# Order of the score blocks and the value projection inside the steps of two cross attentions

## The reference, cut to what matters

```
# second (l1x): masked, scaled dot products      # fourth (l3x): unit vectors and a bias
q, k, v = x@Wq, ctx@Wk, ctx@Wv                   q, k = l2norm(x@Wq + bq) * scale, l2norm(ctx@Wk)
w = where(mask, -1e10, q.k / 4)                  w = q.k + fside            # fside: 64 x 1601
out = softmax(w) @ v @ Wproj + b                 out = softmax(w) @ v @ Wo + b
```

## Time and profile before

| | us |
|---|---|
| median of 3 runs | 2484.82 (2483.24 to 2486.69) |
| the profiled execution, its own time | 2488.87 |
| span of the profiled execution | 2487.2 |
| second cross attention, batches in the loop | about 374 to 695 |
| fourth cross attention, batches in the loop | about 1838 to 2226 |

### The profile page before, as it was taken

How to read it: one execution, slowest core, us unless ns; L and a number is a source line. 1 busy time by engine, 2 the same in 40 slices (tenths; PEclk the granted TensorE clock), 3 DMA queues, 4 the chain that set the end, 5 groups by cost and what they waited for, 6 DMA issues and landing times. The chain is left out here.

```text
span 2487.2 us, 51006 instructions
## 1 busy us (share of the span) xinstructions
PE 2239.6 (90%) x20593; PEld 1421.5 (57%) x20650; DVE 1649.7 (66%) x3182; ACT 1243.9 (50%) x2071; POOL 814.2 (33%) x688
## 2 busy tenths in 40 slices
PE   8885879999978899999999999699879999998898
PEld 6764546666644555666655666356545555566554
DVE  6976365555549746888888854744676666665577
ACT  3335135555554235555555554576545555563565
POOL 5610052242208020332133300045545455443254
PEclk9998889999989989999999999899999999999999
DMA  4201363334231237666686663133322323220231
GB/s 118 73 1 47 100 167 91 95 86 120 54 135 38 47 99 144 132 137 125 141 155 124 115 117 69 34 108 102 110 67 72 83 74 82 68 67 23 72 96 60
DMA packets 358619, 226.84 MB, mean 91 GB/s; under 512 B 289913, under 2 KB 326611, under 8 KB 358387
## 3 DMA queue, kind: packets, MB, share of 16 engines
q1 hardware_dynamic: 355314, 215.20, 35.8%
q0 software_dynamic: 3072, 8.39, 1.2%
HBM read 114.87 MB, written 0.52 MB: 46 GB/s over the span
## 5 line engine op out<-in xcount | busy, mean ns | idle before, releaser
L3953 POOL TENSOR_TENSOR l2x_rows<-l2x_rows,l2x_one 128x256 f16<-128x256 f32 (+1 forms) x91 | 89.2, 1007 | 382.1 <-DVE l2x_rows L1507 354.6
L100 PE MATMUL PS<-hot 128*128 128x512 f16 x460 | 139.6, 441 | 82.4 <-DVE l0a_g L1119 17.5
L4057 PE MATMUL PS<-l2x_rows,l2x_pth 128*128 128x512 f16 x832 | 200.4, 379 | 1.9 <-DVE l2x_mean L4266 1.9
L3714 DVE CUSTOM_DVE_ANT_0 l1x_junk<-PS,l1x_bias 128x1024 bf16<-128x1024 f32 (+1 forms) x128 | 123.3, 992 | 74.3 <-PE PS L3374 73.4
L4259 DVE TENSOR_TENSOR l2x_pl<-l2x_sc,l2x_ph 128x1664 f16<-128x1664 f32 x64 | 125.1, 1954 | 44.6 <-ACT l2x_ph L4136 43.9
L4154 ACT ACTIVATE l2x_meanT<-PS 128x256 f32<-128x256 f32 x64 | 24.6, 384 | 250.3 <-PE PS L4019 250.3
L4244 DVE CUSTOM_DVE_ANT_0 l2x_sc<-PS,l2x_bias 128x1665 f32<-128x1665 f32 x64 | 120.9, 1889 | 38.5 <-issue 37.3
L3714 DVE CUSTOM_DVE_ANT_0 l3x_junk<-PS,l3x_bias 128x1024 bf16<-128x1024 f32 (+1 forms) x128 | 123.6, 991 | 24.2 <-PE PS L3374 21.2
L100 PEld LDWEIGHTS PS<-hot 128*128 128x128 f16 x460 | 45.8, 109 | 153.1 <-issue 39.8
L4011 PE MATMUL PS<-l2x_kh,l2x_qth 128*128 128x512 f16 (+1 forms) x512 | 131.9, 339 | 1.5 <-issue 1.5
L4011 PE MATMUL PS<-l2x_kl,l2x_qth 128*128 128x512 f16 (+1 forms) x512 | 131.9, 339 | 0.0
(11 more groups left out here) (866 smaller groups left out, 6119.4 us busy)
## 6 DMA issues: line engine op xcount, KB each, us to landing
l2f_unit<-in_L_ffn_units_dram SPq DMA_DIRECT2D x36, 384.0 KB, 3.1
l3f_unit<-in_L_ffn_units_dram SPq DMA_DIRECT2D x34, 384.0 KB, 3.1
l1x_kst<-l1x_kh SPq DMA_DIRECT2D x128, 100.1 KB, 2.2
l3x_kst<-l3x_kh SPq DMA_DIRECT2D x128, 100.1 KB, 2.2
l2x_rows<-in_ctx_dram SPq DMA_DIRECT2D x8, 1536.0 KB
l1x_ctx<-in_ctx_t_dram SPq DMA_DIRECT2D x7, 1601.0 KB, 7.6
l3x_ctx<-in_ctx_t_dram SPq DMA_DIRECT2D x7, 1601.0 KB, 7.9
l1x_kst<-l1x_kl SPq DMA_DIRECT2D x64, 100.1 KB, 2.2
```

The lines of the kernel that those rows point to most:

```text
L100: self.nc.tensor.matmul(self.PS[:, bank, :], self.hot[:, 0:P], self.hot[:], start=True, stop=True)
L3714: v.tensor_tensor_reduce(junk[:, slot(it), 0:n], slot_banks(it)[:, 0:n], bias[:, 0 if normed else b % 2, at:at + n], 1.0, LOWEST, ALU.add, ...
L3953: last = nc.gpsimd.tensor_tensor(high[:, at], of[:, at], one[0:p, at].unsqueeze(2).unsqueeze(3).to_broadcast([p, i, NC, P]), ALU.mult)
L4057: nc.tensor.matmul(PS[:, ACC, :], pth[:, u % 2, m, :], rows2[:, b % 2, :, :, m, :], start=(m == 0), stop=False)
```

## The change

The lists of steps are edited, nothing else. In the second attention three pairs [V, A] become [A, V] (steps 10, 13, 16) and [M 0, A10] becomes [A10, M 0] (step 18). In the fourth, A2 moves from step 13 into step 14 ahead of V3, A4 moves from step 15 to step 16, and [M 0, A10] becomes [A10, M 0] (step 20). No instruction is added or removed.

```
     if normed:
...
-                 [P_, A[0], ("U", 1, 1)], [A[1], A[2]], [("V", 3, 0)], [A[3], A[4]], [A[5]], [A[6]], [A[7], A[8]],
-                 [A[9]], [("M", 0, 0), A[10]], [A[11]], [A[12]], [A[13], A[14]], [A[15]], [("M", 1, 0)]]
+                 [P_, A[0], ("U", 1, 1)], [A[1]], [A[2], ("V", 3, 0)], [A[3]], [A[4], A[5]], [A[6]], [A[7], A[8]],
+                 [A[9]], [A[10], ("M", 0, 0)], [A[11]], [A[12]], [A[13], A[14]], [A[15]], [("M", 1, 0)]]
...
     else:
...
-                 [("V", 1, 0), A[2]], [A[3]], [P_, A[4]], [("V", 2, 0), A[5]], [A[6]], [A[7]], [("V", 3, 0), A[8]], [A[9]],
-                 [("M", 0, 0), A[10]], [A[11]], [A[12]], [A[13]], [A[14]], [A[15]], [], [("M", 1, 0)]]
+                 [A[2], ("V", 1, 0)], [A[3]], [P_, A[4]], [A[5], ("V", 2, 0)], [A[6]], [A[7]], [A[8], ("V", 3, 0)], [A[9]],
+                 [A[10], ("M", 0, 0)], [A[11]], [A[12]], [A[13]], [A[14]], [A[15]], [], [("M", 1, 0)]]
```

## The result

| | us |
|---|---|
| before, median of 5 runs | 2484.82 (2483.24 to 2492.22) |
| changed, median of 5 runs | 2496.53 (2493.61 to 2501.92) |
| ratio changed to before | 1.0047, 95% interval 1.0033 to 1.0061 |
| forecast | 2494.5 (2482 to 2501) |

11.7 us were lost; 9.7 were forecast. The profiled execution of the changed kernel took 2501.92 us, the slowest of its five, so its span (2500.2 us) shows 13 us more and not 11.7.

The account below looks back on a forecast made before the run. The prediction took PE, busy 93 to 94%, as the bound. It added 4.4 us (second attention) and 5.3 us (fourth), 9.7 in all, to the median of 2484.8: 2494.5 us, range 2482 to 2501.

Parts of the forecast that it names:

- PE's waits set the pace: Both stages: PE is busy 93 to 94%, so the change is worth the change in PE's waits, no work being added.
- The 1.92 us from the start of a wide A to the next use of its slot: Both attentions: a wide A read by DVE holds its slot 1.92 us from start to start, if DVE is free.
- Second attention: 0.63 a batch, 4.4 us: Second attention: new waits of V2, A9 and A11 make each batch end 0.63 us later, 4.4 us over 7 batches.
- The 0.25 us for a narrow A: PE's time for a narrow A directly ahead of another instruction, estimated at 0.25 us from the wide one's 0.44.
- Fourth attention: A2's wait passes to V3 and nothing is gained: Fourth attention, steps 13 and 14: V3 still starts when DVE has read A1, so A2's wait becomes V3's; gain nothing.
- A4's move costs 0.63 to 0.64, M 0's swap the rest of 0.87: Fourth attention, steps 15 to 21: A6 starts 0.63 us late behind A4's read; by A11 the lateness is 0.87 us.
- The two batches with a DMA wait hide half: Fourth attention: in two of seven batches A8's wait for stacking DMAs takes in lateness, leaving 0.45 us each.
- Exponentials and ACT's later copy cost nothing: ACT gets V's copy 0.44 us later, ahead of an exponential; PE's work covers it, barely; uncovered, some 12 us.
- The lateness is carried on: Both attentions: all later waits hang on PE's own output, so the lateness is not absorbed.
- Rival 1: Both attentions: removed waits simply vanish, no new ones arise; 14.5 us faster, 2470; chance 0.10 together with a weaker form.
- Rival 2: PE's lateness goes into DMA and K waits, time stays at 2485; chance 0.22 together with half the sum, 2489.5.
- Rival 3: Fourth attention: after V3's longer wait the clock falls to 1.2 GHz; 37 us in 14 batches, 2531; chance 0.03.

Follow-up runs that it names:

- the short reads: Changed kernel with DVE's wide reads in the loop batches covering 577 of 1024 columns; two batches take 89.55 us (second attention) and 106.21 us (fourth).
- the repeated run: The same changed kernel measured once more against the kernel before: 2510.24 against 2500.21 us on that chip, ratio 1.0040 (1.0027 to 1.0053).
- the halves: Two kernels, each with the change in one attention only, against the kernel before: second alone 2490.03 us, 1.0023; fourth alone 2489.44 us, 1.0020.

## Why the prediction was right, point by point

- **PE's waits set the pace.** Right. The number of PE's instructions is the same, and each period changed by what its waits changed.
- **The 1.92 us from the start of a wide A to the next use of its slot.** Right: V2 starts at 538.99, A4 at 537.06, 1.93. The run with the short reads shows that it is the cause, and not just a duration that fits: with the order left as changed and the read shortened, V2 starts 1.46 us behind A4 and the loss of the second attention turns into a gain.
- **Second attention: 0.63 a batch, 4.4 us.** Measured 0.62 to 0.64 and 4.6 us; the first batch of the loop lost 0.81 (42.17 to 42.98). Each term held when run alone: A3's -0.63 (-0.64), V2 and A6 +0.65 (+0.65), A9 +0.39 to 0.41 (+0.41), A11 about +0.2 (+0.22). The 0.25 us for a narrow A, an estimate, was good within 0.01.
- **Fourth attention: A2's wait passes to V3 and nothing is gained.** Right, period within 0.01. I took V3's 1.6 us from one batch, though; it holds for four of the seven, and in the other three V3 takes over 0.65. I also took U's 1.90 us as a fixed length; with the short reads it became 2.37, with its end still 0.62 us behind POOL's. **A4's move costs 0.63 to 0.64, M 0's swap the rest of 0.87.** Measured 0.66, 0.25 and together 0.90.
- **The two batches with a DMA wait hide half.** The size was off a little: they lost 0.72 and 0.45 us instead of 0.45 each in the repeated run. The fourth lost 5.9 us, I had 5.3; 0.2 of it is the one late A11.
- **Exponentials and ACT's later copy cost nothing.** Right, no new row of PE's waits names them; what the gap is without cover was not tried.
- **The lateness is carried on.** Right; the halves and the whole show their stage's sum again in the time: 4.6 + 5.9 = 10.5 us in the stages, 11.7, 10.0 and (by halves) 10.3 us in the medians.
- **Rival 1, the removed waits are simply gone.** Wrong: V2's new wait is there, and A2's move by itself gained nothing.
- **Rival 2, absorbed.** It holds for the two DMA batches only. The K waits kept their 9.8 us in 7. I had written that these have the same length in every batch, and under rival 3 that there are seven of 1.6 us; in the trace there are six of 1.58 and one of 0.33.
- **Rival 3, the clock.** It happened, once in seven batches of one execution, and cost about 1.6 us and not 37. Whether it belongs to the change is the question of the last section.

What the forecast lacked was small: 9.7 against 11.7 (10.0 in the repetition). About 0.8 us of it are found in the stages; the rest is inside the scatter of the runs, and that the medians came this close to a sum of such small terms is in part luck.

## What to carry to other kernels

When two PSUM slots are handed round in turn, write down for every item who had its slot before and how long that reader holds it, from start to start (here 1.92 us for a wide block read by DVE, 1.51 from its end for one copied by ACT); an order is good where the work between two users of a slot is at least that long. A long matmul group directly behind a wide A helps, as its 24 matmuls cover the read of that block before its slot comes round (V1 behind A2); one item later it hurts, as it then needs the wide A's slot itself (V2 behind A4 and A5). A row that vanishes from the table of waits is no gain until the period of the loop has become shorter.

## What the runs showed of the hardware that I had not expected

The granted clock fell inside the loop of the fourth attention. In the changed kernel, V3 waits 1.57 us until 1947.16; the window before has PE busy for 1.63 of 3.20 us at a clock of 1.00, the next 3.40 us have 0.52, the 1.2 GHz level, both shown at the top. The rows there come to be twice as far apart as in other batches (0.42 us for two matmuls of 256 columns instead of 0.22):

```profile
1947.16 0.53 PE L3363 MATMUL PS<-l3x_wh,l3x_ctxh 128*65 128x256 f16 x2 [1.57 <-DVE l3x_rmax L3714]
1947.48 0.63 PE L3363 MATMUL PS<-l3x_wl,l3x_ctxh 128*65 128x256 f16 x2
1947.90 0.63 PE L3363 MATMUL PS<-l3x_wh,l3x_ctxl 128*65 128x256 f16 x2
```

It is not the new order's doing alone. The kernel with V2's swap, whose fourth attention is as before, shows the same in the same batch, behind two waits of 0.6 and 0.8 us:

```profile
1940.00:1944.00 4.00, 3.42 (x15) 1.94 (x15) 2.28 (x5) 1.62 (x4) 3.84 (x5) 0.58 0.07 17
```

That batch took 54.73 us from M 1 to M 1 (46.73 + 8.00), where the same one before took 53.54.

All profiled executions together say more. The clock fell seven times inside the loop of the fourth attention, always at V3's wait, and never inside that of the second. Three falls were behind a wait of 1.57 us: one each in the changed kernel, with A2's move and with the short reads, in five executions with four such waits each. Four were behind the two waits of 0.64 and 0.76 us of the old order: one each with V2's and V3's swap and two with M 0's, in nine executions with four such pairs each. That is 3 in 20 and 4 in 36, too few to tell apart. So a fall is possible at this spot in either order; in the changed kernel it cost 1.6 us (55.81 against 54.26), with V3's swap 1.5 (54.46 against 52.99) and with V2's 1.2. Whether the longer wait makes it more frequent stays open.

The length of a wait alone doesn't decide it: K(1,1)'s 1.58 us in the second attention stand six times in each of twelve executions, and the clock fell behind none of them.

The other surprise is the key multiply U in the fourth attention. Its smaller form (128x577) takes from 0.98 to 2.37 us, 1.90 ahead of V3's wait of 1.57 us, where the larger one (128x1024) ahead of it takes 1.23. In the traces of the kernel before, the changed one and the one with the short reads, all 14 of the smaller form run beside an instruction of POOL's key split and end 0.61 to 0.63 us behind its end, whenever they started. The multiply waits for a signal of ACT and for none of POOL in between; no run here tested by what POOL holds it up. For the reader of a timeline it means that the length of such a row is partly waiting, and that work moved ahead of it on DVE may bring nothing.
